# Joining the two halves of each value product in the loop of a cross-attention and expert kernel

## The reference

```python
x = x + xattn(layernorm(x), ctx)          # x, ctx: 32 x 64 x 512, fp32
  q = (x_norm @ Wq + bq)                  # 32 heads of 128, in 8 groups of 4
  k, v = split(ctx @ Wkv + bkv)           # 8 key heads of 128
  attn = softmax(q k^T / sqrt(128))       # within each of the 32 sequences
  o = attn @ v;  return o @ Wo + bo
x = x + ffn(layernorm(x))                 # 8 low-rank experts of rank 16, the best 2 of each token
```

## Time and profile before

| | |
|---|---|
| time before, median of 3 runs (lowest to highest) | 1066.92 us (1066.81 to 1067.96) |
| profiled execution: its time, its span | 1070.41 us, 1068.2 us |
| busy in the span: PE, DVE, POOL, ACT | 1038.2, 805.1, 674.2, 557.2 us |
| mean granted TensorE clock | 0.992 |

### The profile page before, as it was taken

One profiled execution on the slowest core, in us unless ns is written; L12 is line 12 of the kernel. 1 busy time (PEld: TensorE's weight loads), 2 busy tenths in 40 slices (PEclk: granted clock), 3 DMA queues, 4 the chain that ended last, 5 costly groups with the idle time before them and its releaser, 6 DMA issues.

```text
span 1068.2 us, 17316 instructions
## 1 busy us (share of the span) xinstructions
PE 1038.2 (97%) x5409; PEld 852.4 (80%) x5409; DVE 805.1 (75%) x1420; ACT 557.2 (52%) x1314; POOL 674.2 (63%) x563
## 2 busy tenths in 40 slices
PE   8999999989999999999999999999999999999996
PEld 6788887767888888888888888888888888887884
DVE  4454355459987888798779878887887797788986
ACT  3032203247766675666567566656665565565420
POOL 0285337758876786678678757876786677584300
PEclk9999999999999999999999999999999999999998
DMA  8636963986382736365463728264654547250013
GB/s 306 197 121 207 340 202 106 366 287 238 110 320 91 284 114 247 141 216 216 147 243 110 283 93 311 98 255 142 222 177 186 209 144 256 100 158 11 2 40 118
DMA packets 85657, 197.99 MB, mean 185 GB/s; under 512 B 10560, under 2 KB 43368, under 8 KB 70384
## 3 DMA queue, kind: packets, MB, share of 16 engines
q1 hardware_dynamic: 83072, 181.73, 48.9%
q10 hardware_dynamic: 2544, 15.73, 3.7%
HBM read 161.78 MB, written 35.65 MB: 185 GB/s over the span
## 4 chain that ended last, share of the span: by engine, by line
PE 83%; DVE 6%; DMA 5%; POOL 2%; issue 1%; ACT 1%; SPq 1%; ACTq 0%; DVEq 0%
PE banks L1673 25%; PE banks L1674 23%; PE banks L1675 23%; PE banks L1813 5%; PE banks L1796 3%; PE banks L1797 3%; DMA values_dram<-parts 2%; DMA v_raw<-values_dram 1%; PE banks L1698 1%; DMA keys_dram<-parts 1%; DVE stats L1229 1%; DMA raw<-in_L_xattn_Wq_dram 1%; POOL w_l L590 1%; DMA parts<-in_L_xattn_bkv_dram 1%; POOL wo_l L590 0%
## 5 line engine op out<-in xcount | busy, mean ns | idle before, releaser
L1673 PE MATMUL banks<-wo_h,xo 128*128 128x512 f32 x512 | 205.1, 401 | 0.0
L1674 PE MATMUL banks<-wo_l,xo 128*128 128x512 f32 x512 | 200.9, 392 | 0.0
L1675 PE MATMUL banks<-wo_h,xo 128*128 128x512 f32 x512 | 200.4, 391 | 0.0
L590 POOL TENSOR_TENSOR qT_l<-parts,qT_h 128x512 fp32r<-128x512 f32 x128 | 165.2, 1297 | 52.8 <-ACT qT_h L817 52.8
L1673 PE MATMUL banks<-xo,w_h 128*128 128x512 f32 x448 | 178.9, 399 | 4.7 <-ACT parts L875 4.7
L1674 PE MATMUL banks<-xo,w_h 128*128 128x512 f32 x448 | 175.6, 392 | 0.0
L1675 PE MATMUL banks<-xo,w_l 128*128 128x512 f32 x448 | 174.4, 389 | 0.0
L590 POOL TENSOR_TENSOR xo<-sT,xo 128x512 fp32r<-128x512 f32 (+1 forms) x72 | 102.5, 1423 | 75.5 <-ACT xo L817 75.5
L1154 DVE TENSOR_TENSOR xo<-banks,xo 128x512 fp32r<-128x512 f32 (+1 forms) x156 | 100.8, 665 | 25.2 <-ACT xo L817 24.6
L1302 DVE SCALAR_TENSOR_TENSOR parts<-banks,g_bias,parts 128x512 f32<-128x512 f32 x128 | 94.7, 741 | 28.6 <-PE banks L1675 26.2
L1673 PEld LDWEIGHTS banks<-wo_h,xo 128*128 128x128 f32 x512 | 96.9, 189 | 23.6 <-issue 0.4
(11 more groups left out here) (145 smaller groups left out, 2274.6 us busy)
## 6 DMA issues: line engine op xcount, KB each, us to landing
xo<-x_dram SPq DMA_DIRECT2D x105, 1024.0 KB, 5.0
x_dram<-xo ACTq DMA_DIRECT2D x14, 1024.0 KB, 11.6
values_dram<-parts SPq DMA_DIRECT2D x64, 128.0 KB, 2.5
keys_dram<-parts SPq DMA_DIRECT2D x32, 256.0 KB, 4.5
k_raw<-keys_dram SPq DMA_DIRECT2D x32, 256.0 KB, 4.9
raw<-in_L_xattn_Wo_dram SPq DMA_DIRECT2D x8, 1024.0 KB, 8.0
v_raw<-values_dram SPq DMA_DIRECT2D x64, 128.0 KB, 4.0
raw<-in_L_xattn_Wkv_dram SPq DMA_DIRECT2D x7, 1024.0 KB, 6.6
```

Source lines behind the costliest of these rows:

```text
L590: return nc.gpsimd.tensor_tensor(dst, src, high_part.bitcast(F32), ALU.subtract)
L1673: mm(dst, stat[0], mov[0], start=start, stop=False)
L1674: mm(dst, stat[0], mov[1], start=False, stop=False)
L1675: return mm(dst, stat[1], mov[0], start=False, stop=stop)
```

## The change

In `duo`, the two halves of a value product are written one right behind the other on PE. They can't share the two `turn` banks then: half c = 0 of unit 2d-2 goes to the score banks `att`, half c = 1 of unit 2d-1 to ring slots 0 and 1, the other two stay in `turn`. Projections get slots by the table `OUT_SLOTS`, products count from slot 0 in every duo, and the waits follow the new owners of the banks. ACT's and DVE's copies of unit 2d-1 stand in another order, with half c = 1 earlier. Opening and tail keep theirs.

```diff
+OUT_SLOTS = (2, 3, 2, 3, 0, 1, 2, 3)
+PV_SLOTS = (0, 1)
...
+        def value_bank(d, k, c, i):
+            if d is not None and k == 0 and c == 0:
+                return att[:, i, :]
+            if d is not None and k == 1 and c == 1:
+                return ring[:, PV_SLOTS[i], :]
+            return turn[:, i, :]
...
@@ scalar, duo @@
                 query_high(d, "c22", 1)
-                output_high(2 * d - 1, 0, 0)
-                output_high(2 * d - 1, 0, 1)
+                output_high(2 * d - 1, 0, 0, d, 1)
+                output_high(2 * d - 1, 0, 1, d, 1)
+                output_high(2 * d - 1, 1, 0, d, 1)
                 swap_max(2 * d, 1)
                 exponents(2 * d, 0)
+                output_high(2 * d - 1, 1, 1, d, 1)
                 keys_high(2 * d + 1)
-                output_high(2 * d - 1, 1, 0)
-                output_high(2 * d - 1, 1, 1)
                 swap_sum(2 * d, 0)
...
@@ vector, duo @@
-                output_low(2 * d - 1, 0, 0)
-                output_low(2 * d - 1, 0, 1)
-                add(2)
+                output_low(2 * d - 1, 0, 0, d, 1)
+                output_low(2 * d - 1, 0, 1, d, 1)
+                output_low(2 * d - 1, 1, 0, d, 1)
                 s_peak(2 * d, 1)
                 s_sum(2 * d, 0)
+                output_low(2 * d - 1, 1, 1, d, 1)
+                add(2)
                 if split:
                     combine_w(g + 1, 1, False)
-                output_low(2 * d - 1, 1, 0)
                 add(3)
                 if split:
                     combine_w(g + 1, 2, False)
                 s_inverse(2 * d, 0)
-                output_low(2 * d - 1, 1, 1)
...
@@ tensor, scores @@
+                if k == 0 and c == 0 and not opening_duo(d):
+                    pe.wait_ge(o_low, (2 * d - 2) * 4 + 2)
...
@@ tensor, outputs @@
-                if not isinstance(u, int) or u > 0 or c > 0:
+                if d is not None and k == 0 and c == 0:
+                    pe.wait_ge(s_added, u * 2 + 4)
+                elif d is not None and k == 1 and c == 1:
+                    for r in range(2):
+                        pe.wait_ge(summed, d * len(SUMS) + SUM_AT["c12", r])
+                elif d is not None:
+                    pe.wait_ge(o_low, u * 4)
+                elif not isinstance(u, int) or u > 0 or c > 0:
...
@@ tensor, out @@
-                if j < 4:
+                if j < 2 or j < 4 and opening_duo(d):
                     pe.wait_ge(summed, d * len(SUMS) + SUM_AT[("c22", "c12")[j // 2], j % 2])
+                elif opening_duo(d):
+                    pe.wait_ge(y_added, d * 8 - 8 + j - 4 + 1)
+                elif j in (4, 5):
+                    pe.wait_ge(o_low, (2 * d - 1) * 4 + 3 + j - 4)
                 else:
-                    pe.wait_ge(y_added, d * 8 - 8 + j - 4 + 1)
-                out_project(2 * d - 2 + j // UT, out_slot(p, j), j % UT)
+                    pe.wait_ge(y_added, d * 8 - 8 + (j - 2 if j < 4 else j - 4) + 1)
+                out_project(2 * d - 2 + j // UT, out_slot(d, p, j), j % UT)
...
@@ tensor, duo @@
-                outputs(2 * d - 2, 0)
+                outputs(2 * d - 2, 0, d, 0)
+                outputs(2 * d - 2, 1, d, 0)
                 product(g, p, 2, 0)
...
                 product(g, p, 4, 0)
-                outputs(2 * d - 2, 1)
                 product(g, p, 4, 1)
...
                 scores(d, 0, 1)
-                outputs(2 * d - 1, 0)
+                outputs(2 * d - 1, 0, d, 1)
+                outputs(2 * d - 1, 1, d, 1)
                 out(d, p, 2)
                 out(d, p, 3)
-                outputs(2 * d - 1, 1)
                 out(d, p, 4)
```

More of the change, by code:

```diff
@@ L348, in start_slot, with opening_duo, product_slot, out_slot @@
             return (n - FIRST_UNIT) % RING
[L350 to L356, removed]
+        def opening_duo(d):
+            return isinstance(d, int) and d < DUOS
+        def product_slot(d, p, k, r):
+            return ((DUO_TASKS * p if opening_duo(d) else 0) + PROD_AT[k, r]) % RING
+        def out_slot(d, p, j):
+            return (DUO_TASKS * p + len(PROD) + j) % RING if opening_duo(d) else OUT_SLOTS[j]
+        def value_bank(d, k, c, i):
[4 more added lines that the diff above has]
+            return turn[:, i, :]
         def high_at(d, c, r):
@@ L874, in first_product @@
                     act.wait_ge(q_low, d * 8 - 4)
-                act.copy(slot_of("x", r), ring[:, product_slot(p, 1, r), :]).then_inc(copied, 1)
+                act.copy(slot_of("x", r), ring[:, product_slot(d, p, 1, r), :]).then_inc(copied, 1)
             def query_high(d, c, r):
@@ L895, in values_high, with output_high @@
                 high(v_h[:], v_raw[:]).then_inc(v_high, 1)
-            def output_high(u, c, i):
+            def output_high(u, c, i, d=None, k=None):
                 act.wait_ge(o_filled, u * 4 + 2 * c + i + 1)
@@ L902, in output_high @@
                 high(out_rows_of(oT_h, c, i),
-                     turn[:, i, :].rearrange("p (n h l) -> p n h l", n=2, l=L)).then_inc(o_high, 1)
+                     value_bank(d, k, c, i).rearrange("p (n h l) -> p n h l", n=2, l=L)).then_inc(o_high, 1)
             def swap(dst, src, blocks):
@@ L1036, in duo @@
                 wo_high_part(2)
-                output_high(2 * d - 2, 0, 0)
-                output_high(2 * d - 2, 0, 1)
+                output_high(2 * d - 2, 0, 0, d, 0)
+                output_high(2 * d - 2, 0, 1, d, 0)
                 query_high(d, "c11", 0)
@@ L1044, in duo @@
                 swap_sum(2 * d - 1, 1)
-                output_high(2 * d - 2, 1, 0)
+                output_high(2 * d - 2, 1, 0, d, 0)
                 query_high(d, "c21", 0)
-                output_high(2 * d - 2, 1, 1)
+                output_high(2 * d - 2, 1, 1, d, 0)
                 values_high(2 * d - 1)
@@ L1263, in product_of @@
                 dve.wait_ge(prod_filled, d * len(PROD) + PROD_AT[k, r] + 1)
-                return ring[:, product_slot(p, k, r), :]
+                return ring[:, product_slot(d, p, k, r), :]
             def made(d, name, r):
@@ L1349, in add_out, with output_low @@
                 nc.vector.tensor_tensor(y[:, t, :], ring[:, slot, :], y[:, t, :], ALU.add).then_inc(y_added, 1)
-            def output_low(u, c, i):
+            def output_low(u, c, i, d=None, k=None):
                 dve.wait_ge(o_high, u * 4 + 2 * c + i + 1)
-                low(out_rows_of(oT_l, c, i), turn[:, i, :].rearrange("p (n h l) -> p n h l", n=2, l=L),
+                low(out_rows_of(oT_l, c, i), value_bank(d, k, c, i).rearrange("p (n h l) -> p n h l", n=2, l=L),
                     out_rows_of(oT_h, c, i)).then_inc(o_low, 1)
@@ L1419, in opening @@
                 dve.wait_ge(resid_ready, TILES)
-                add_out(0, 0, 0, out_slot(1, 0))
-                add_out(0, 0, 1, out_slot(1, 1))
+                add_out(0, 0, 0, out_slot(1, 1, 0))
+                add_out(0, 0, 1, out_slot(1, 1, 1))
                 s_inverse(1, 1)
@@ L1436, in opening @@
                 output_low(1, 1, 1)
-                add_out(0, 0, 2, out_slot(1, 2))
+                add_out(0, 0, 2, out_slot(1, 1, 2))
                 s_inverse(2, 0)
@@ L1441, in opening @@
                 p_turn(2, 0)
-                add_out(0, 0, 3, out_slot(1, 3))
-                add_out(1, 1, 0, out_slot(1, 4))
-                add_out(1, 1, 1, out_slot(1, 5))
+                add_out(0, 0, 3, out_slot(1, 1, 3))
+                add_out(1, 1, 0, out_slot(1, 1, 4))
+                add_out(1, 1, 1, out_slot(1, 1, 5))
                 s_inverse(2, 1)
@@ L1447, in opening @@
                 p_turn(2, 1)
-                add_out(1, 1, 2, out_slot(1, 6))
+                add_out(1, 1, 2, out_slot(1, 1, 6))
                 combine_w(1, 4, False)
                 s_max(3, 0)
-                add_out(1, 1, 3, out_slot(1, 7))
+                add_out(1, 1, 3, out_slot(1, 1, 7))
                 s_add(3, 1)
@@ L1459, in add @@
                 def add(j):
-                    add_out(2 * d - 2 + j // UT, (2 * p + 2) % UNITS + j // UT, j % UT, out_slot(p, j))
+                    add_out(2 * d - 2 + j // UT, (2 * p + 2) % UNITS + j // UT, j % UT, out_slot(d, p, j))
                 if p == 0:
@@ L1472, in duo @@
                 query_sum(d, p, "c11", 1)
-                output_low(2 * d - 2, 0, 0)
-                output_low(2 * d - 2, 0, 1)
+                output_low(2 * d - 2, 0, 0, d, 0)
+                output_low(2 * d - 2, 0, 1, d, 0)
                 s_inverse(2 * d - 1, 0)
@@ L1484, in duo @@
                 w_sum(d, p, 1)
-                output_low(2 * d - 2, 1, 0)
+                output_low(2 * d - 2, 1, 0, d, 0)
                 query_sum(d, p, "c22", 1)
@@ L1488, in duo @@
                 add(0)
-                output_low(2 * d - 2, 1, 1)
+                output_low(2 * d - 2, 1, 1, d, 0)
                 p_turn(2 * d - 1, 1)
@@ L1627, in _ @@
                 elif kind == "y":
```

(11 more changed lines are left out.)

## The result

The changed kernel takes **1089.38 us** (median of 4 runs, 1087.55 to 1092.65), the kernel before, run beside it on the same chip, 1067.44 us: a ratio of **1.0205, interval 1.0183 to 1.0228**. It is slower. Its time lies 0.4% above the 1085.5 us forecast and inside the range.

A forecast was written before the change was run, and what follows sets the result against it. PE, busy 97% of the span, was taken to bound the kernel. The terms -10.9 + 24.8 + 4.2 + 0.9 = +19.0 us gave 1085.9, say 1085.5 us, range 1074 to 1097.

The forecast's parts named there:

- The saving: Joined value-product halves on PE: 0.39 us saved at each of 28 joins, 10.9 us, bounds 5.5 and 14.
- what a joined half saves: Prediction step pricing a half: 0.19 us at its own edges plus 0.20 at the matmul behind, 0.39 us.
- The stall: PE waits at out(d, p, 4) for the moved copy behind out(d, p, 3): 1.77 us a duo, 24.8 us in 14.
- Late behind it: Work behind the waiting copy delays scores(d, 1, 1) in six split duos: 0.7 us each, 4.2 us, bounds 0 to 8.4.
- The last duo: Sums of layernorm after add(5) on DVE come later and set the end: 0.9 us once, bounds 0 and 2.
- What cost nothing: New waits for score banks, c12 sums, probability splits and key loads: all covered, put at nothing.
- the clock: Rival 1: PE's clock falls after the new stalls; 1097 if after half of the 14, 1108 if all; 10%.
- Rivals 2 and 4: Rival 2: shorter wait, nothing late behind, 1076 or 1073, 10%. Rival 4: the 0.39 us gaps stay, 1097, 4%.
- Rival 3: Only the saving remains, 1056; needs output_high(2d-1, 1, 0) not to wait; decides below a 0.78 us stall a duo; 4%.

The follow-up runs named there:

- the fast version: The change with unit 2d-1's half c = 1 in ring slots 2 and 3, projections 2 to 5 in other slots, ACT's copies back behind the keys: 1054.94 us.
- The first join: The kernel before with only the halves of unit 2d-2 joined, the first in the score banks: 1063.12 us, ratio 0.9928.
- The second: The join of unit 2d-1's halves; run alone as the change with the halves of unit 2d-2 apart again: 1095.75 us, ratio 1.0239.
- the change with its copies back: The change with ACT's copies of half c = 1 behind exponents and keys again, DVE's first low part behind the sum: 1080.84 us, ratio 1.011.

## Why the prediction was right

The mechanism was right in each step that carried the sum. Three sizes were off: the saving by 2.5 us one way, the stall and the waits behind it by 1.1 and 1.4 us the other way. They nearly cancel, so that the sum came out within half a microsecond was luck.

1. *The saving*, predicted 28 x 0.39 = 10.9, measured 28 x 0.48 = 13.4. The step mis-sized is "what a joined half saves": it counted the half's edges and the first matmul behind, and put nothing for the ten matmuls after that, which start up to 0.06 us late in all. (The 0.20 that it put at the matmul behind is right as a sum. The chain counts from end to end; by the starts 0.09 of it lies ahead of the half, where the last 128-row matmul takes 522.54 - 522.22 = 0.32 us to the next start.) The upper bound of 14 held it.
2. *The stall*, predicted 14 x 1.77 = 24.8, measured 14 x 1.85 = 25.9. The chain PE, ACT, DVE, PE took 583.21 - 581.27 = 1.94 from start to start against 1.89 from the tail, and showed as 1.55 idle, as said. The first matmul behind it took 583.54 - 583.21 = 0.33 to the next start, against 0.34 in the earlier trace rows.
3. *Late behind it*, predicted 6 x 0.7 = 4.2, measured 6 x 0.93 = 5.6. The place, the engine and the idle time were right (0.66 to 0.69 us in five of the six, 0.95 in one). The term took the idle time for the loss. As at the stall, 0.25 to 0.3 us come on top: the last matmul ahead counts as busy for 0.39 us, where the next would start after 0.23, and the first matmuls behind start 0.10 to 0.14 us late in all. `s_add` ended 595.98 - 581.27 = 14.71 us after the projection's last matmul, with 14.5 predicted.
4. *The last duo*, predicted 0.9, measured 792.1 - 772.8 - (25.9 + 5.6 - 13.4) = 1.2. The size was right and the place was not: the tail's scores and value product wait longer, and not the sums of layernorm. A wait of 0.56 with 0.26 on top, and 1.92 - 1.68 = 0.24 more at the product, are 1.06 of the 1.2. The rows, to be held against 983.70 in the earlier trace rows:

```profile
1001.26 0.36 PE L1812 MATMUL banks<-qT_h,kT 128*128 128x256 f32 x1 [0.56 <-DVE sT L1326]
...
1005.86 0.39 PE L1836 MATMUL banks<-xo,v_h 64*128 64x256 f32 x2 [1.92 <-DVE xo L1168]
```

5. *What cost nothing* cost nothing: no value product in the loop waits for score banks or sums, and `out(d, p, 5)` has no second stall.

Together -13.4 + 25.9 + 5.6 + 1.2 = 19.3, with 19.0 predicted. That the last term is what was left over makes this sum close by itself; the other three were measured apart. The measured median lies 3.9 us above the forecast, 0.5 of it because the kernel before took 1067.44 and not 1066.92 beside it; by the ratios of the two measurements, 1.0205 and 1.0182, the change is worth 19.4 to 21.9 us. What more than 19.3 there is of that I put down to nothing: the openings of two profiles of the changed kernel alone differ by 298.25 - 293.87 = 4.4 us.

Of the rivals, the clock did not fall in the loop: in 700 us of the loop, with its stalls, the granted clock (third from the end) is 1.00.

```profile
300.00:1000.00 700.00, 674.15 (x3582) 559.01 (x3583) 578.73 (x954) 424.24 (x1040) 495.43 (x406) 1.00 0.51 181
```

Rivals 2 and 4 fall with the stall's 1.85 and the join's 0.48. Rival 3 is what the fast version does, at 1054.94 where 1056 was given. Its condition was put too strictly, though: the copy need not stop waiting for `out(d, p, 3)`. It is enough that neither PE's next matmul nor ACT's next work needs it.

## What to carry to other kernels

Where an engine that sets the time is fed by an in-order list, ask of each moved instruction what it waits for on arrival, not only what it produces: a 0.6 us copy whose wait was met before now held ACT for 3.7 us. What that costs depends on what stands behind it: in the change itself the waits that went when it was put back were some 6.6 us, and in the fast version the same place alone cost 25, as much as the new chain through the banks. The first join paid as it was, 0.7%. The second is worth having only with slots and places in the lists chosen so that nobody needs the late copy; then both joins gave 1.5%. To price many small waits, measure the time of one round of the loop: each wait of this loop cost 0.25 to 0.3 us more than the idle time it shows.

## What was not expected of the hardware

The clock. The tail's idle stretch of 1.68 us ahead of a value product is in the kernel before, and was followed there by the granted clock 0.50. At the same place, the changed kernel (1.92 us idle) and the change with its copies back (1.68) show this (rows over 3.3 us, from 0.6 us behind the first matmul):

```profile
1006.50:1009.80 3.30, 3.30 (x15) 2.50 (x13) 3.22 (x6) 2.23 (x6) 0.00 (x0) 0.64 0.00 0
```

```profile
995.79 0.38 PE L1836 MATMUL banks<-xo,v_h 64*128 64x256 f32 x2 [1.68 <-DVE xo L1168]
```

```profile
996.40:999.70 3.30, 3.30 (x20) 2.58 (x18) 3.22 (x6) 2.49 (x7) 0.00 (x0) 1.00 0.00 0
```

After the same 1.68 us of idle time, the same work ran at 1.2 GHz in the kernel before (granted clock 0.50, 14 matmuls in the row) and at 2.4 GHz throughout in the change with its copies back (1.00, 20 matmuls). The next product of the tail starts 16.35 us later in the one (1000.05 after 983.70) and 14.83 in the other (1010.62 after 995.79). Of the eleven profiles, seven show the clock fallen there, to 0.50 to 0.65 over such a row, and four show 1.00, with 1.68 and with 1.92 us of idle time in both groups. So 1.5 us depend on something that the length of the stretch alone doesn't tell. No run here shows what.
